# A recommendation kernel with look-ups on TensorE: weights turned on chip, transposed moves in six transfers, four look-ups per tile instead of three, and fewer low-part matmuls

## What is computed

```python
emb = embed_table[f_ix, x_idx]                       # n x 26 x 16
lin1 = w1_table[f_ix, x_idx].sum(axis=1, keepdims=True) + w1_bias
fm = 0.5 * ((s * s).sum(-1) - (emb * emb).sum(axis=(1, 2)))[:, None]      # s = emb.sum(axis=1)
h = relu(emb.reshape(n, F * D) @ mlp_w1 + mlp_b1)    # 416 -> 400
h = relu(h @ mlp_w2 + mlp_b2)                        # 400 -> 400
mlp_out = h @ mlp_w3 + mlp_b3
for W in (cin_w0, cin_w1, cin_w2):                   # x0 = emb transposed, last starts as x0
    last = jnp.einsum('ndl,ndf,klf->ndk', last, x0, W)
    feats.append(last)
return lin1 + fm + mlp_out + jnp.concatenate(feats, axis=-1).sum(axis=1) @ lin_w + lin_b
```

## Time and profile before

| | before |
|---|---|
| median of 3 runs | 530.52 us (530.1 to 530.93) |
| the profiled execution | 530.45 us |
| its span | 528.6 us, mean granted TensorE clock 0.968 |
| PE, PEld busy | 468.6 us (89%), 384.6 us |
| DVE, ACT busy | 376.7 us (71%), 361.6 us (68%) |
| POOL busy | 364.6 us (69%) |

### The profile page before, as it was taken

How to read it: one execution, slowest core, us unless ns; L and a number is a source line. 1 busy time by engine, 2 the same in 40 slices (tenths; PEclk the granted TensorE clock), 3 DMA queues, 4 the chain that set the end, 5 groups by cost and what they waited for, 6 DMA issues and landing times. The chain is left out here.

```text
span 528.6 us, 6627 instructions
## 1 busy us (share of the span) xinstructions
PE 468.6 (89%) x2230; PEld 384.6 (73%) x2230; DVE 376.7 (71%) x610; ACT 361.6 (68%) x707; POOL 364.6 (69%) x382
## 2 busy tenths in 40 slices
PE   0798499899898989899999989898989899998895
PEld 0795367588787878687877878787868687787684
DVE  6811265869687786868686968778686868695766
ACT  1002459878686877777676868786777767677883
POOL 5777787877777777777777777777777777774000
PEclk9999559899999999999999999999999999999998
DMA  8973652122222222222222222222222222221000
GB/s 179 237 133 26 82 132 8 5 8 7 9 7 9 7 8 7 9 7 9 7 8 7 8 8 8 8 8 8 8 8 8 8 8 7 8 8 6 0 2 1
DMA packets 21550, 13.63 MB, mean 26 GB/s; under 512 B 12792, under 2 KB 20493, under 8 KB 21261
## 3 DMA queue, kind: packets, MB, share of 16 engines
q0 software_dynamic: 12064, 3.31, 18.4%
q1 hardware_dynamic: 5863, 7.92, 6.4%
q10 hardware_dynamic: 3590, 1.99, 2.0%
HBM read 13.00 MB, written 0.19 MB: 25 GB/s over the span
## 5 line engine op out<-in xcount | busy, mean ns | idle before, releaser
L417 POOL DMA_INDIRECT emb<-rows,idx_raw x377 | 364.3, 966 | 117.4 <-issue 114.6
L660 DVE TENSOR_TENSOR z_lo<-ps_s,z_hi 128x512 fp32r<-128x512 f32 (+1 forms) x192 | 130.7, 687 | 66.5 <-ACT ps_s L483 65.1
L476 ACT ACTIVATE z_hi<-ps_s 128x512 fp32r<-128x512 f32 (+1 forms) x192 | 114.4, 596 | 78.7 <-PE ps_s L908 77.8
L483 ACT ACTIVATE ps_s<-ps_s 128x512 f32<-128x512 f32 (+1 forms) x192 | 113.9, 593 | 0.7
L922 PE MATMUL ps_q<-z_lo,zw_hi 128*127 128x512 f32 (+1 forms) x192 | 86.0, 448 | 15.9 <-DVE z_lo L660 14.4
L923 PE MATMUL ps_q<-z_hi,zw_lo 128*127 128x512 f32 (+1 forms) x192 | 76.4, 398 | 0.0
L924 PE MATMUL ps_q<-z_hi,zw_hi 128*127 128x512 f32 (+1 forms) x192 | 76.3, 397 | 0.0
L908 PE MATMUL ps_s<-xt,pick 128*128 128x512 f32 (+1 forms) x192 | 74.3, 402 | 0.4 <-DVE xt L652 0.4
L922 PEld LDWEIGHTS ps_q<-z_lo,zw_hi 128*127 128x127 f32 (+1 forms) x192 | 36.4, 190 | 32.4 <-DVE z_lo L660 19.7
L994 PE MATMUL ps_y<-look_hi,one_hot 128*128 128x442 f32 (+1 forms) x156 | 56.3, 361 | 2.3 <-DVE one_hot L754 2.3
L995 PE MATMUL ps_y<-look_lo,one_hot 128*128 128x442 f32 (+1 forms) x156 | 54.8, 353 | 0.0
(11 more groups left out here) (165 smaller groups left out, 757.2 us busy)
## 6 DMA issues: line engine op xcount, KB each, us to landing
emb<-rows,idx_raw POOLq DMA_INDIRECT x377, 3.0
w_space<-rows SPq DMA_DIRECT2D x2, 728.9 KB
m_raw<-mlp_w SPq DMA_DIRECT2D x2, 650.0 KB
w<-cin_w SPq DMA_DIRECT2D x1, 832.0 KB, 6.7
w<-cin_w ACTq DMA_DIRECT2D x1, 832.0 KB, 13.2
w_space<-cin_w SPq DMA_DIRECT2D x1, 832.0 KB, 15.0
w_space<-cin_w ACTq DMA_DIRECT2D x1, 832.0 KB, 18.4
m_raw<-rows SPq DMA_DIRECT2D x1, 728.9 KB
```

Source lines behind the costliest of these rows:

```text
L417: pool.indirect_dma_start(emb[t % EMB][:, f, :], None, rows, bass.IndirectOffsetOnAxis(row_ix[:, t, f:f + 1], 0)).then_inc(gathered[t], 16)
L476: act.activation(z_hi[0:k, c, :], ps[0:k, :], ACT.Square)
L483: act.activation(ps[0:k, :], ps[0:k, :], ACT.Square).then_inc(hi_ready, 1)
L660: dve.tensor_tensor(z_lo[0:k, u % NC, :], ps_s[s_no(t, u) % RING][0:k, :], z_hi[0:k, u % NC, :].bitcast(F32), ALU.subtract).then_inc(lo_re ...
```

## The change

**Weights.** cin_w2 and cin_w1 come in quarters. ScalarE and VectorE copy each so that the 128 weights of a matmul lie side by side (`turn`), and TensorE takes 64 of them at a time, so that it can begin with the first half. **Moves.** The blocks are stored already in the order in which they are read, by six stores, and `move` is one transfer for each of six blocks instead of 53. **Keys.** The matmuls `keys` are gone: all keys are transposed once in start-up and come back by one transfer per tile into `key_row`. **Look-ups.** Four fields are looked up instead of three, so that 22 rather than 23 fields are gathered for tiles 3 to 15, and `one_hot` has two buffers. **Layer 1.** The low parts of the weights of two blocks stand in one matmul (`x_two`, four matmuls instead of eight), the copy `x32` is made later (`x_full`), and layer 2 has ten matmuls. **Memory.** `emb` has three buffers, not four; several tiles share space. **Last tile.** Its copy is in two parts, and TensorE transposes it behind the whole of tile 14.

```diff
-LOOKS = 3
+LOOKS = 4
 FIRST_LOOK = 3
 LEAD = 2
+EARLY = 18
...
-        LOOK_SPLIT = {4: 0, 6: 1, 8: 2}
-        KEYS = {1: 0, 5: 1, 9: 2}
-        ROWS = {3: 0, 7: 1, 11: 2}
-        PICKED = {5: 0, 9: 1}
+        LOOK_SPLIT = {3: 0, 5: 1, 7: 2, 9: 3}
+        KEYS = {3: 0, 5: 1, 8: 2, 10: 3}
+        ROWS = {3: 0, 6: 1, 8: 2, 11: 3}
+        PICKED = {6: 0, 9: 1, 11: 2}
 
         CONSTS = 15
-        MOVES = [N1 + N1 + N1 + 2, N2 + N2 + 2, N3 + 2]
+        MOVES = [3 + 2, 2 + 2, 1 + 2]
...
+        def leave(eng, n):
+
+            name, g, c0, col, ab, n_b, n_c, n_d = BLOCKS[n]
+            n_a, here = GROUPS[g], {"y12": y12, "y13": y13, "y23": y23}[name]
+            run = n_c * n_d
+            order = [[run, n_a], [n_a * run, n_b]] if ab else [[run, n_b * n_a]]
+            eng.dma_start(bass.AP(y_dram[n].tensor, y_dram[n].offset, order + [[1, run]]),
+                          here[:, c0:c0 + run]).then_inc(y_stored[n], 16)
...
+        def move(eng, n):
+
+            name, g, c0, col, ab, n_b, n_c, n_d = BLOCKS[n]
+            n_a = GROUPS[g]
+            eng.wait_ge(y_stored[n], 16)
+            eng.dma_start(moved[0:n_a * n_c, g, col:col + n_b * n_d].rearrange("p (b d) -> p b d", d=n_d),
+                          bass.AP(y_dram[n].tensor, y_dram[n].offset,
+                                  [[n_d, n_a * n_c], [n_a * n_c * n_d, n_b], [1, n_d]])).then_inc(moved_in[g], 16)
...
+            sp.wait_ge(keys_stored, 16)
+            for n in range(3, 6):
+                sp.wait_ge(y_stored[n], 16)
+            for t in range(FIRST_LOOK, T):
+                if t >= FIRST_LOOK + 2:
+                    sp.wait_ge(one_hot_ready, look_no(t - 2, LOOKS))
+                sp.dma_start(key_row[t % 2], key_dram[LOOKS * t:LOOKS * (t + 1), :].partition_broadcast(P)
+                             ).then_inc(keys_in[t % 2], 16)
...
-                                            ).then_inc(gathered[t], 16)
+                                            ).then_inc(gathered[t] if t < T - 1 or f < EARLY else gathered_late, 16)
...
+            for h in range(2):
+                act.wait_ge(w2_in[h], 16 * 2)
+                act.activation(turned(w2_turn, h, 0), turning(w2[:], h, 0), ACT.Copy).then_inc(w2_turned[h], 1)
...
+            def copy_last_early():
+                act.wait_ge(gathered[T - 1], 16 * EARLY)
+                act.wait_ge(looked, look_no(T - 1, LOOKS))
+                for fs in (slice(0, EARLY), slice(F - LOOKS, F)):
+                    act.activation(by_pos[:, :, fs], emb[(T - 1) % EMB][:, fs, 0:D].rearrange("p f d -> p d f"), ACT.Copy)
+
+            def copy_last_late():
+                fs = slice(EARLY, F - LOOKS)
+                act.wait_ge(gathered_late, 16 * (F - LOOKS - EARLY))
+                act.activation(by_pos[:, :, fs], emb[(T - 1) % EMB][:, fs, 0:D].rearrange("p f d -> p d f"),
+                               ACT.Copy).then_inc(by_pos_ready, 2)
...
-                act.activation(x32[t % 2][LO * h:LO * h + XR], ps, ACT.Copy)
                 act.activation(xt[t % 2][0:XR, 4 * h:4 * h + 4, :], ps, ACT.Copy).then_inc(hi_ready, 1)
+
+            def x_pairs(t):
+                act.activation(x_two[0:XR], xt[t % 2][0:XR, 0:C8:2, :].bitcast(F32), ACT.Copy)
+                act.activation(x_two[LO:XK], xt[t % 2][0:XR, 1:C8:2, :].bitcast(F32), ACT.Copy).then_inc(x_two_ready, 1)
+
+            def x_full(t, h):
+                act.wait_ge(lo_ready, x_no(t, h) + 1)
+                act.activation(x32[t % 2][LO * h:LO * h + XR],
+                               ps_s[x_no(t, h) % RING][0:XR, :].rearrange("p (c n) -> p c n", c=4),
+                               ACT.Copy).then_inc(x32_ready, 1)
...
             def start_tile(t):
                 x_high(t, 0)
                 x_high(t, 1)
-                for u in range(NC):
-                    square(t, u)
+                square(t, 0)
+                x_full(t, 0)
+                x_full(t, 1)
+                square(t, 1)
+                square(t, 2)
+                x_pairs(t)
+                sum_first(t)
...
+            def turn(here, raw, in_sem, out_sem, h):
+                dve.wait_ge(in_sem[h], 16 * 2)
+                dve.tensor_scalar(turned(here, h, 1), turning(raw, h, 1), 1.0, None, ALU.mult).then_inc(out_sem[h], 1)
+
...
                     if looks(t + LEAD):
                         if u in PICKED:
                             pick_row(t + LEAD, PICKED[u])
-                        if u - 2 in KEYS:
-                            keys_to_one_hot(t + LEAD, KEYS[u - 2])
+                        if u in KEYS:
+                            keys_to_one_hot(t + LEAD, KEYS[u])
...
+            def start_last():
+                t = T - 1
+                times_left(t - 1, NQ - 1)
+                times_third(t - 1)
+                add_third(t - 1)
+                add_product(t - 1, NQ - 1)
+                fold(t - 1)
+                hidden2(t - 1)
+                x_low(t, 0)
+                x_low(t, 1)
+                for u in range(NC):
+                    z_low(t, u)
 
...
                 add_third(t - 1)
+                if looks(t - 1 + LEAD):
+                    pick_row(t - 1 + LEAD, LOOKS - 1)
                 z_low(t, 0)
                 add_product(t - 1, NQ - 1)
                 z_low(t, 1)
                 fold(t - 1)
                 hidden2(t - 1)
-                if looks(t - 1 + LEAD):
-                    pick_row(t - 1 + LEAD, 2)
                 z_low(t, 2)
...
             def keys_to_one_hot(t, i):
-                dve.wait_ge(keys_out, look_no(t, i) + 1)
-                dve.tensor_tensor(one_hot[:], ps_y[:, 0:P].unsqueeze(1).to_broadcast([P, SHARES, P]),
+                if i == 0:
+                    dve.wait_ge(keys_in[t % 2], 16 * ((t - FIRST_LOOK) // 2 + 1))
+                n = look_no(t, i)
+                if n >= 2:
+                    dve.wait_ge(rows_out, n - 1)
+                dve.tensor_tensor(one_hot[n % 2][:], key_row[t % 2][:, i:i + 1, :].to_broadcast([P, SHARES, P]),
                                   share_row.unsqueeze(2).to_broadcast([P, SHARES, P]),
                                   ALU.is_equal).then_inc(one_hot_ready, 1)
...
-            for g in range(F):
-                mm = pe.matmul(ps_y[:, g:g + 1], w2[:, :, g], lin[:, 2:3], start=True, stop=True)
+            for h in range(2):
+                ls = slice(HALF_P * h, HALF_P * (h + 1))
+                pe.wait_ge(w2_turned[h], 2)
+                for g in range(F):
+                    mm = pe.matmul(ps_y[ls, g:g + 1], w2_turn[:, g, ls], lin[:, 2:3], start=True, stop=True)
             mm.then_inc(m_done, 1)
...
+                if u in (1, 2):
+                    pe.wait_ge(x32_ready, 2 * t + u)
...
-                for c in range(C8):
-                    mm = pe.matmul(ps_mlp[:, 0:H], x[0:96, c, :], m1_lo[0:96, c, :], start=False, stop=(c == C8 - 1))
+                pe.wait_ge(x_two_ready, t + 1)
+                for c in range(C8 // 2):
+                    mm = pe.matmul(ps_mlp[:, 0:H], x_two[0:XK, c, :], m1_lo[0:XK, c, :], start=False,
+                                   stop=(c == C8 // 2 - 1))
...
-                for c in range(4):
-                    kb = HC + (c == 3)
-                    pe.matmul(ps_mlp[:, 0:H], h1t_lo[0:HC, c, :], m2_hi[0:HC, c, :], start=(c == 0), stop=False)
-                    pe.matmul(ps_mlp[:, 0:H], h1t_hi[0:kb, c, :], m2_lo[0:kb, c, :], start=False, stop=False)
-                    mm = pe.matmul(ps_mlp[:, 0:H], h1t_hi[0:kb, c, :], m2_hi[0:kb, c, :], start=False, stop=(c == 3))
+                for c in range(3):
+                    pe.matmul(ps_mlp[:, 0:H], h1t_lo[:, c, :], m2_hi[:, c, :], start=(c == 0), stop=False)
+                    pe.matmul(ps_mlp[:, 0:H], h1t_hi[:, c, :], m2_lo[:, c, :], start=False, stop=False)
+                    pe.matmul(ps_mlp[:, 0:H], h1t_hi[:, c, :], m2_hi[:, c, :], start=False, stop=False)
+                mm = pe.matmul(ps_mlp[:, 0:H], h1t_rest[:], m2_rest[:], start=False, stop=True)
...
-            def keys(t, i):
-
-                n = look_no(t, i)
-                if n == 0:
-                    pe.wait_ge(look_step, 10)
-                if n:
-                    pe.wait_ge(looked, n)
-                pe.matmul(ps_y[:, 0:P], look_key[:, t, i:i + 1].to_broadcast([P, P]), ident,
-                          start=True, stop=True).then_inc(keys_out, 1)
 
             def look_rows(t, i):
                 n = look_no(t, i)
                 if n < LOOKS:
                     pe.wait_ge(look_lo_ready, i + 1)
+                if n:
+                    pe.wait_ge(looked, n)
                 pe.wait_ge(one_hot_ready, n + 1)
...
-                        if u in KEYS:
-                            keys(t + LEAD, KEYS[u])
                         if u in ROWS:
                             look_rows(t + LEAD, ROWS[u])
-                    if after is not None:
+                    if after is not None and after < T - 1:
...
+                    if after == T - 1:
```

(7 more changed lines are left out.)

318 lines of the change are left out of this document (202 added, 116 removed).

## The result

The changed kernel takes **532.73 us** (median of 6 runs, 532.43 to 533.04); the kernel before took 530.60 us beside it (530.10 to 531.08). The ratio is 1.0041, with a 95% interval of 1.0031 to 1.0051: 0.4% slower. The prediction was 521 us, 1.8% faster, with 511 to 528 as its range. It is wrong in sign and in size.

What follows compares the result with a forecast made beforehand. TensorE's chain of waits was taken as the bound, GpSimd's gathers almost abreast: 123.2 + 12 x 28.5 = 465.2, then 17.9 + 0.75 + 12.95 + 22.1 gives 518.9; with 1.85 around it 521 us, range 511 to 528.

Steps and rivals of the forecast that it cites:

- I need not know, because something else ends later: Start-up: whether turned weights save nothing or up to 12 us was left open; the last moved group at 47 to 48 us decides.
- From the last group to the first main matmul: Start-up: 10 to 13 us with only a third of 18 matmuls left, so first main matmul at 57 to 61 us.
- start-up late: Rival, 1 in 10: moves or tables cost more, first main matmul at 64 to 67 us, time 524 to 527.
- Tile 2 bound by its gathers: Tile 2: gathers land at 112.8 us, then copies and look-up; it begins at 123.2 us, 9.9 us earlier than before.
- The tile with look-ups: Tiles with look-ups: waits followed round one tile sum to 28.5 us against 28.56, range 28.3 to 28.8.
- the fourth look-up gives nothing: Tiles with look-ups: the extra look-up costs nothing and gives nothing on TensorE, 28.5 us against 28.56.
- rival 1: Rival, 3 in 10: TensorE's waits vanish and the gathers set the end, 512 to 513 us.
- Comparisons and gathers: GpSimd: four comparisons with two SBUF tensors hold gathers 0.18 us each, 0.7 per tile, making 28.2 us per tile.
- the rival of 0.52 us for each comparison: Rival, 5 in 100: comparisons stall gathers by up to 0.68 us each; from 0.52 us on, slower than before.
- The end: Tiles 14 and 15: late transposes put everything in series, step 2 starts 12.95 us after step 11, costing 5.4 us.
- the 1.1 that it took off tile 14: Tile 14, start to step 11: 1.1 us less for two transposes and a wait, part of 21.3 becoming 17.9.
- a longer tile: Rival, 5 in 100: picks at steps 6 and 11 bind as well, a tile 0.3 to 0.8 us longer, 525 to 531.

Runs made afterwards that it cites:

- c3b: Changed kernel with the six moves of pairs issued as 53 small transfers again, stores left as they are: 541.52 us, ratio 1.0208 to the kernel before.
- a3: Changed kernel with ScalarE's start order mended: SP issues all cin_w1 transfers, w1 is turned before the wait for m; 527.65 us, ratio 0.9959 to the kernel before.
- c2b: Changed kernel with the edits of a1, a3 and a4, plus ScalarE's first x_full copy ahead of the first square: 509.94 us, ratio 0.9631.
- c1b: Changed kernel with the edits of a1, a3 and a4, but three look-ups and 23 gathers per tile: 527.35 us, ratio 0.9926.
- a4: Changed kernel with each tile's second pick on VectorE one step earlier, ahead of z_lo of step 9: 525.97 us, ratio 0.9919 to the kernel before.
- a1: Changed kernel with tile 15 treated like every other tile again, transposed during tile 14, one copy by position: 526.73 us, ratio 0.9935 to the kernel before.
- b3: Changed kernel with each comparison as four operations of one SBUF tensor and one number per partition: 537.03 us, ratio 1.0131 to the kernel before.

## Why the prediction was wrong

**Start-up: the step "I need not know, because something else ends later" failed.** It let ScalarE's copy and moves start when the gathers of tile 0 land, at 38 us, and so put the last group at 47 to 48. The copy stood at 47.29, behind the y blocks, that is behind m and b; in the trace of before it had stood there already, at 46.93, and I had read only the gathers. The moves were sized rightly (5 to 6 us of issue; 48.48 to 53.8 measured, and they carry 7.7 us by c3b), but they start 9 us later than assumed. And what I had dismissed, when TensorE begins, is what it all hangs on: a3 takes 4.8 us out of b and gets them back at the end. The turned weights, for which I had up to 12 us, gain 1.1 for m and lose more to ScalarE's order. From the last group to the first main matmul I had 10 to 13 us, with TensorE free when it comes; it took 14.2. TensorE was not free: it was working off the matmuls by row at half clock, and those of the third group start at 60.02, 3.6 us after its addition. The rival "start-up late" (64 to 67 us) was still too early against 70.64.

**Tile 2 bound by its gathers: wrong.** Its first half was transposed at 123.8 us, TensorE's own time; the gathers had been there for 12 us. Step 0 of tile 2 came at 131.85, forecast 123.2. Tile 0 took 32.2 us, as forecast (32); what was wrong is the start that I counted it from, 58 instead of 70.64. Whether the gathers bind tile 2 once the start-up is ready by 61 us, no run here shows: the earliest first main matmul is at 65.62 (c2b).

**The tile with look-ups: right.** Forecast 28.5, measured 28.50, with 0.8 us of waiting at the third look-up, forecast 0.9, released by the pick. It is not luck: in tile 13 the terms are 5.0, 2.1, 7.1, 7.6 and 6.8 us, where the sum had 4.9, 2.0, 7.1, 7.6 and 6.9. The statement that the fourth look-up gives nothing holds only for the order as written. c1b shows it is what allows a period under the gathers' 29.05, and a4 and c2b show that 0.54 and 0.36 us of the period were avoidable waits. My rival 1, waits gone and gathers the end, did not occur either: with both waits mended a tile takes 27.60.

**Comparisons and gathers: right in mechanism, the size a little low.** 0.7 us per tile forecast, 1.0 measured (0.25 for each comparison, not 0.18), and the rival of 0.52 us for each comparison stayed far. The gathers were never waited for in the change.

**The end: right in mechanism, the term mis-sized.** From the start of tile 14 to the end I had 53.7 us and it took 57.2. The largest part of the gap is the passage from step 11 of tile 14 to step 2 of tile 15, forecast 13.7 (0.75 and 12.95), measured 16.0; the stretches before and behind it are 0.7 and 0.6 us too short. Against a1 the late transposes cost 6.4 us by the traces and 5.6 by the times, where the sum had 5.4, and 4.3 after the 1.1 that it took off tile 14 for them. What was missing is the clock: it falls in TensorE's pause of 2.23 us, 3.0 us of the 6.4 are work at the lower level, and I took every duration in that stretch from rows at the upper one.

Taken together: tile 2 is 8.7 us later than forecast, the middle exact, the end 3.6 too short, 12.3 us; the forecast span was 518.9 and the measured one 531.1. With 6 in 100 for slower I had no case in which the gain of the start-up is small *and* the known cost at the end stays. What I had on the slower side was about gathers and a longer tile, where the real case is plain: by the table everything else gains 4.0 us, and the passage to tile 15 costs 6.5.

## What to carry to other kernels

When a step "ends later anyway", look at where it stood in the trace of before, not only at the input that I think it waits for; here one row at 46.93 us spoke against 38. An edit that feeds TensorE faster through a copy on another engine is worth what that engine's order allows: read its queue, the issues of transfers and the table load included. And a pause written into TensorE's stream can cost more than its own length: here 3.4 us of waits brought 3.0 us of work at the lower clock with them, which is a reason to give it other work even in the last tile.

## What the runs showed of the chip

**Comparisons of two SBUF tensors hold gathers.** In the changed kernel 29 of the 217 gathers issued between 170 and 450 us last over 0.99 us, up to 1.43. All of them begin while a comparison of two SBUF tensors runs on VectorE and end 0.82 us after it. In the whole trace 52 gathers begin in one of the 52 comparisons: the 39 that begin 0.07 us or more behind its start end 0.82 us after its end, the 13 that begin 0.02 us behind its start take their 0.94 or 0.95 us. The subtraction of the earlier trace rows held its gather in the same way, also until 0.82 us after its end. Before, where the comparison read PSUM and SBUF, none of 225 did. In b3, with one SBUF tensor and a number per partition, 3 of 225 do, by 0.1 us at most. "SBUF — State Buffer" of the Trainium skill, section "Who interferes with whom", infers that a VectorE operation with two SBUF inputs does not hold descriptor generation. These traces show the opposite.

**b3's form contends too.** The same section says that a form like b3's can take the pair of ports that VectorE shares with GpSimd, if its operands meet certain conditions. b3's trace does not speak against that. All 41 of its small operations that start 0.50 to 0.66 us behind the start of a gather end 0.99 us behind it, just behind the gather's end, and take 0.34 to 0.49 us where one away from gathers takes 0.28: here VectorE waits for the gather. Gathers are held too. In four cases an operation that began 0.07 to 0.14 us before a gather ends 0.15 to 0.21 us after the gather's start, and the gather ends 0.82 us after the operation, as with the long comparisons; that makes it 0.02 to 0.09 us longer. Two that begin 0.08 us after the start of an operation are not held. By the same 0.82 us an operation that is over 0.12 us after a gather's start costs it nothing, and with operations of 0.28 us that is the usual case. So b3 does not show that the kind of operands sets the gathers free; that the short operations do it is argued, since one operation of 512 columns in this form was not run. At the same length of 0.68 us only one thing is shown, by the kernel before: with one of the two tensors in PSUM no gather is held.

**GpSimd falls into step with TensorE.** It waits for no semaphore in the tiles with look-ups, yet its period is that of TensorE: 22 gathers without a hold take 27.5 us, and the holds add 1.0 us per tile in the change (period 28.50), 0.5 in a4 (27.96) and 0.1 in c2b (27.60). In c2b 25 of the 39 gathers that meet a comparison begin within 0.03 us of its start and are not held; in the change 13 of 52. A comparison that comes at another time against the gathers holds the next one for longer or not at all, until the two keep time. b3 speaks for it: with the holds gone GpSimd leaves the step, 27.5 us per tile beside TensorE's 28.71. How the two find their distance is argued from these traces and was not tried by itself.

**Strided weights.** With 128 columns and a stride of 26 a matmul with one moving column took 0.229 us, with 64 columns 0.111, and turned 0.104. So it was the width that took the time, and the stride 7% at 64 columns. A turned matmul of 128 columns was not run.
